# Channel products as 64-row tiles, the channel mix as four 64x64 tiles, shrinkage in 1024-column instructions

## The chip, the cores and the metric

One core of one Trainium2 chip. The metric is the device time of one launch, in microseconds (us), the median of several runs. Engines: TensorE (PE in the rows, its weight loads PEld), VectorE (DVE), ScalarE (ACT), GpSimd (POOL), SyncE (SP, which issues most DMAs here). A kernel that is better has a lower time.

## The reference

Four layers are applied to `x` of shape (8, 64, 256, 256) in float32: 8 images, 64 channels, 256 by 256 pixels.

```
# layer 0: channel attention
att = einsum('bcn,bdn->bcd', q, q)                  # the Gram matrix, q = x as (b, 64, 65536)
x   = gamma * einsum('bcd,bdn->bcn', softmax(max(att) - att), q) + x
# layers 1 and 3: a long convolution with a separable filter, plus bias * x
# layer 2: Haar wavelet, two branches of channel product and soft shrinkage, inverse Haar
f1 = haar2d(x)
for i in range(2):
    f4  = einsum('bchw,oc->bohw', f1 * v[i], conv_w[i])
    acc = acc + sign(f4) * relu(abs(f4) - tau[i])
x = haar2d(acc, inverse=True) + x
```

The convolution filters come from a small network of three sine layers, which the kernel evaluates once at its start.

## The kernel before

The images go one after the other through two kinds of stage, each of 64 steps (one per channel, or one per group of 8 image rows). `timeline` writes their order by hand: mix of image 0; forward stage -1; mix of image 1; six times a forward stage with all three parts (`fwd`, `shrink`, `gram`) and an inverse stage with mix; a forward stage without Gram (stage 6); an inverse stage without mix; `last_shrink`; a last inverse stage. `quads` unrolls four steps into a loop body and lets parts of one step work on items of earlier steps (`on[k]` is the part with lag k). All engines run the same step list and meet at counting semaphores; `CR` is an offset of 5.

**Forward stage.** In each step TensorE does, for the next image, two Toeplitz products of the first convolution (`toeplitz`, L464 and L466), a full forward Haar of one axis (`haar_fwd`, L474) and a half Haar of the other (`haar_halves`, L490, in fp32r). For the present image it multiplies the coefficients by the two channel matrices: `product(a)` for a = 0, 1 (L538). Each is two float32 matmuls whose stationary operand is 128 x 128, that is 64 channels x 2 row halves in partitions and 128 pixels as columns, and whose moving operand is `chan_w`, 128 x 256. That operand is block-sparse: `chan_w` holds each weight once per row half and a zero for the other half. `turn` (L549) transposes the same pixels with `eye`, since layer 2 adds its input. Four matmuls of a Gram product per step (L442) stand in two halves, one behind `product(1)` and one behind the second Toeplitz product. Every float32 matmul shows as two records in the trace, each with its own weight load; a transpose shows as one.

The shrinkage of a step is a chain over four engines. Before, each of its links works on one bank of 512 columns at a time: `scale(a)` (DVE, L941, multiplies by `v`), `absolute(a)` (ACT, L721, back into PSUM), `sign(a)` (ACT, L725), `less(a)` (DVE, L948, subtracts `tau` in PSUM), `relu(a)` (ACT, L730, into `mag`), magnitude times sign (POOL, L1089), the sum of the two branches (POOL, L1092, into `pair_sum`), and `field` (DVE, L971), which adds the transposed input. `product(a)` waits for `relu` of that bank from the step before; `turn` waits for `field` of the step before. ACT also evacuates the Toeplitz result into `mid` (L735), which frees bank 0 for the next step's first Toeplitz product; writes `split_b` (L756, `f_hi`), which waits for the half Haar of that step; and copies `res` (L769). DVE also makes `x1` (L980), the low part of `split_b` (L985) and two one-row corrections (L960, L961).

**Inverse stage.** Per step one fp32r inverse Haar (L482), a half Haar (L490) and two Toeplitz products. Where `mix` is on, 64 matmuls a stage (`mix_one`, L615) apply the attention matrix to the image after next: stationary `mix_w`, 128 x 128 and block-sparse in the same way, moving 512 pixels. ACT copies each result (L799) into one of two buffers and sends it to DRAM. `mix_one(m)` waits for the copy of m - 2, so the two banks alternate. Every 12 steps hold 16 of these, one or two in a step.

**last_shrink** does products, turns and shrinkage of the last image with nothing beside them. Its vector instructions have 1024 columns already (L1055, L844, L846, L1070, L841, L1116), only the branch sum (L1120) and `field` (L1064) have 512. Its products are L665.

Of the kernel before, what the change touches and what calls it, by code (L numbers as in the profile page):

```python
# [22 lines left out]
F32 = mybir.dt.float32  # L23
# [6 lines left out]
C = 64  # L30
# [87 lines left out]
def build(nc, x_pix, x_rows, gamma, zt, w1, w23, wo, b123, freq, bias, v, tau, cw, decay, signs_fwd, signs_inv,  # L118
# [4 lines left out]
    with ctx:  # L123
# [7 lines left out]
        coef = nc.dram_tensor("coef", (B, C, H, 2 * N), F32, kind="Internal").ap()  # L131
        mixed = nc.dram_tensor("mixed", (C, H, 2 * N), F32, kind="Internal").ap()
# [12 lines left out]
        held = sb("held", [128, 2, 512])  # L145
        sgn = sb("sgn", [128, 2, 512], BF16)
# [8 lines left out]
        mix_w = sb("mix_w", [128, 2 * C])  # L155
        chan_w = sb("chan_w", [128, 4 * C])
# [90 lines left out]
        def _(sp):  # L247
# [22 lines left out]
            def load_img(c, d):  # L270

                src = mixed[bass.ds(c, 1), :, :].rearrange("o p n -> p (o n)")
                sp.dma_start(img[:, d].rearrange("p a n -> p (a n)"), src).then_inc(img_in[d], 16)

            def load_coef(b, chunk, buf):

                rows_of = coef[bass.ds(b, 1), :, :, :].rearrange("o c (s t) n -> (o c s) (t n)", s=2)
# [52 lines left out]
            def inverse_stage(b, inv, mix):  # L330
                if mix:
# [3 lines left out]
                    if inv:  # L335
                        sp.wait_ge(c_pair, 128 * b + 128 + CR)
                        sp.nop(nofuse=True)
                        sp.wait_ge(c_sign, 128 * b + 128 + CR)
# [90 lines left out]
        def _(pe):  # L429
# [76 lines left out]

            def inverse_width(n, bank):
# [6 lines left out]
            def forward_stage(b, fwd, shrink, gram):  # L514
# [11 lines left out]
                def step(q, j, on):  # L526
# [3 lines left out]
                    def product(a):  # L530
                        src = crows[j // 2]
                        if j % 2 == 0 and a == 0:
                            pe.wait_ge(crows_in[j // 2], 16 * (16 * b + q) + 16)
                        pe.wait_ge(c_relu, 2 * (64 * b + d) + a - 1 + CR)
                        o_ps = ps[:, 4 + a, :].rearrange("p (i c h) -> p i c h", i=2, h=4)
                        for t in range(2):
                            at = 512 * t + N * a + H * (j % 2)
                            mm = nc.tensor.matmul(o_ps[:, :, :, 2 * t:2 * t + 2], src[:, at:at + H], chan_w[:, :],  # L538
                                                  start=True, stop=True)
                        mm.then_inc(c_mm, 1)  # L540

                    def turn():
                        src = crows[j // 2]
                        pe.wait_ge(c_field, 64 * b + d + CR)
                        for a in range(2):
                            o_ps = ps[:, 6, N * a:N * a + N].rearrange("p (c h) -> p c h", h=4)
                            for t in range(2):
                                at = 512 * t + N * a + H * (j % 2)
# [644 lines left out]
```

## Time and profile before

| | |
|---|---|
| runs | 6577.37, 6580.49, 6584.24 us; median 6580.49 us |
| the profiled execution | 6581.41 us in all, span 6579.6 us |
| TensorE busy | 6266.2 us, 95% of the span |
| mean granted clock of TensorE | 0.983 of full speed |
| VectorE, ScalarE, GpSimd busy | 61%, 59%, 39% |

The profile shows one execution. "Span" runs from the first to the last instruction. A step of a forward stage with all three parts takes 7.04 us, so a tenth of a microsecond in each of the 384 such steps is 38 us of the kernel.

### The profile page before, as it was taken

To read this page: it belongs to the slowest core of one execution; us is meant where nothing else is said; L and a number is where in the kernel's file an instruction comes from. 1 tells how busy PE (TensorE), PEld (TensorE's weight loads), DVE (VectorE), ACT (ScalarE), POOL (GpSimd) and SP (SyncE) were. 2 spreads that over 40 slices of the span, in tenths; PEclk is the share of its full clock that TensorE was granted. 3 is DMA by queue.
4 is the path that set the end of the run, shared out by engine and by line. 5 is a ranking of instruction groups with operands and counts; after the bars stand their busy time and mean duration, and the time that the engine had idled before them with its cause. 6 is when DMAs were issued, how large, how long until landed. Compare 5 with 4: busy or idle time off the path is not lost.

```text
span 6579.6 us, 140048 instructions
## 1 busy us (share of the span) xinstructions
PE 6266.2 (95%) x37984; PEld 5474.9 (83%) x37984; DVE 4017.5 (61%) x7165; ACT 3907.0 (59%) x7001; POOL 2553.6 (39%) x2436
## 2 busy tenths in 40 slices
PE   6798799999999999999999999999999999999689
PEld 4496599889998899888998889988998889988579
DVE  1142377556775577755776567755677558866866
ACT  0233466556665566655666566655666557755865
POOL 0000255324552255423553245532455226633952
PEclk9899899999999999999999999999999999999999
DMA  6676656575556655576555766666655665534224
GB/s 197 220 215 209 209 185 188 183 232 184 187 176 205 218 186 185 164 234 203 187 186 177 234 189 185 187 189 219 190 188 174 217 202 169 172 123 141 74 86 129
DMA packets 770784, 1216.81 MB, mean 185 GB/s; under 512 B 78855, under 2 KB 475048, under 8 KB 770569
## 3 DMA queue, kind: packets, MB, share of 16 engines
q1 hardware_dynamic: 623112, 945.68, 48.4%
q10 hardware_dynamic: 147456, 268.50, 10.8%
q8 instruction: 106, 1.74, 0.1%
q14 instruction: 110, 0.89, 0.0%
HBM read 808.13 MB, written 405.73 MB: 184 GB/s over the span
## 4 chain that ended last, share of the span: by engine, by line
PE 90%; DMA 4%; ACT 2%; DVE 2%; issue 1%; POOL 1%; SPq 0%; ACTq 0%; DVEq 0%; POOLq 0%
PE ps L464 27%; PE ps L466 14%; PE ps L538 12%; PE ps L482 7%; PE ps L490 7%; PE ps L474 7%; PE ps L442 7%; PE ps L615 5%; DMA mixed<-x 3%; PE ps L549 3%; PE ps L665 1%; DMA pix<-in_x_pix 1%; ACT x L799 1%; DVE pix L1055 1%; DVE ps L1070 1%
## 5 line engine op out<-in xcount | busy, mean ns | idle before, releaser
L1089 POOL TENSOR_TENSOR mag<-mag,sgn 128x512 f32<-128x512 f32 x896 | 1039.3, 1160 | 2124.0 <-ACT mag L730 2093.3
L1104 POOL TENSOR_TENSOR split_a<-field,split_a 128x512 fp32r<-128x512 f32 x512 | 651.3, 1272 | 1751.5 <-ACT split_a L782 1751.5
L464 PE MATMUL ps<-tab_a,img 128*128 128x256 f32 x4096 | 1226.5, 381 | 14.5 <-DMA img<-mixed 8.2
L464 PE MATMUL ps<-tab_b,mid 128*128 128x256 f32 x4096 | 1224.3, 381 | 0.4 <-DVE x L980 0.4
L941 DVE TENSOR_TENSOR held<-ps,v_t 128x512 f32<-128x512 f32 x896 | 619.8, 692 | 601.5 <-PE ps L538 560.5
L466 PEld LDWEIGHTS ps<-tab_a,img 128*128 128x128 f32 x4096 | 781.2, 191 | 107.4
L466 PEld LDWEIGHTS ps<-tab_b,mid 128*128 128x128 f32 x4096 | 778.8, 190 | 105.4
L466 PE MATMUL ps<-tab_a,img 128*128 128x128 f32 x4096 | 789.2, 274 | 0.0
L466 PE MATMUL ps<-tab_b,mid 128*128 128x128 f32 x4096 | 787.3, 274 | 0.0
L464 PEld LDWEIGHTS ps<-tab_a,img 128*128 128x128 f32 x4096 | 700.0, 192 | 88.6 <-DMA img<-mixed 8.5
L482 PE MATMUL ps<-s_inv,split_a 128*128 128x256 f32 x4096 | 704.2, 315 | 38.0 <-issue 37.7
L482 PEld LDWEIGHTS ps<-s_inv,split_a 128*128 128x128 f32 x4096 | 546.9, 192 | 187.9 <-issue 178.6
L1092 POOL TENSOR_TENSOR pair_sum<-mag 128x256 f32<-128x256 f32 x896 | 650.5, 726 | 103.9 <-POOL mag L1089 66.6
L756 ACT ACTIVATE split_b<-ps 128x512 fp32r<-128x512 f32 x512 | 305.7, 597 | 618.5 <-PE ps L490 609.9
L799 ACT ACTIVATE x<-ps 128x512 f32<-128x512 f32 x512 | 305.9, 598 | 586.4 <-PE ps L615 406.2
L442 PE MATMUL ps<-pix 128*128 128x128 f32 x4096 | 614.0, 277 | 26.0 <-DMA pix<-in_x_pix 26.0
L464 PEld LDWEIGHTS ps<-tab_b,mid 128*128 128x128 f32 x4096 | 627.2, 192 | 3.9 <-issue 0.6
L985 DVE TENSOR_TENSOR split_b<-ps,split_b 128x512 fp32r<-128x512 f32 x512 | 354.1, 692 | 452.4 <-ACT split_b L756 450.7
L782 ACT ACTIVATE split_a<-field 128x512 fp32r (+1 forms) x512 | 322.6, 630 | 502.6 <-PE ps L482 434.7
L948 DVE TENSOR_TENSOR ps<-ps,tau_t 128x512 f32<-128x512 f32 x896 | 619.4, 691 | 1.5 <-ACT ps L721 1.4
L735 ACT ACTIVATE mid<-ps 128x512 f32<-128x512 f32 x512 | 305.6, 597 | 520.8 <-PE ps L466 520.8
L442 PEld LDWEIGHTS ps<-pix 128*128 128x128 f32 x4096 | 564.0, 193 | 52.5 <-DMA pix<-in_x_pix 30.9
(101 smaller groups left out, 11118.1 us busy)
## 6 DMA issues: line engine op xcount, KB each, us to landing
pix<-in_x_pix SPq DMA_DIRECT2D x256, 512.0 KB, 3.8
mixed<-x ACTq DMA_DIRECT2D x512, 256.0 KB, 3.3
img<-mixed SPq DMA_DIRECT2D x512, 256.0 KB, 2.7
tab_a<-filt SPq DMA_DIRECT2D x1024, 128.0 KB, 2.8
tab_b<-filt SPq DMA_DIRECT2D x1024, 128.0 KB, 2.8
out<-res SPq DMA_DIRECT2D x512, 256.0 KB, 3.4
coef<-res ACTq DMA_DIRECT2D x496, 256.0 KB, 2.0
pix<-in_x_rows SPq DMA_DIRECT2D x128, 512.0 KB, 5.0
```

Source lines behind the costliest of these rows:

```text
L442: mm = nc.tensor.matmul(ps[:, 7, 0:2 * C], pix[:, buf, j, :], pix[:, buf, j, :], start=False, stop=False, skip_group_check=True)
L464: nc.tensor.matmul(o_ps, src[:, 0, H * half:H * half + H], tab[:, N - 1::-1], start=True, stop=False)
L466: mm = nc.tensor.matmul(o_ps[:, H:N], src[:, 1, H * half:H * half + H], tab[:, N - 1:H - 1:-1], start=False, stop=True)
L474: mm = nc.tensor.matmul(o_ps, src[:, kh, H * half:H * half + H], s_fwd[:, kh, :].bitcast(F32), start=(kh == 0), stop=(kh == 1), skip_group ...
L482: mm = nc.tensor.matmul(ps[:, bank, N * half:N * half + N], src[:, piece, kh, H * half:H * half + H], s_inv[:, kh, :], start=(kh == 0 and ...
L490: mm = nc.tensor.matmul(ps[:, bank, :], signs[:, :], src[:, piece].rearrange("p a n -> p (a n)"), start=(piece == 0), stop=(piece == 1))
L538: mm = nc.tensor.matmul(o_ps[:, :, :, 2 * t:2 * t + 2], src[:, at:at + H], chan_w[:, :], start=True, stop=True)
L941: nc.vector.tensor_tensor(held[:, a].rearrange(grouped, i=2, h=4), ps[:, 4 + a, :].rearrange(grouped, i=2, h=4), table(v_t, a), ALU.mult)\
L948: nc.vector.tensor_tensor(bank, bank, table(tau_t, a), ALU.subtract).then_inc(c_less, 1)
L1089: nc.gpsimd.tensor_tensor(mag[:, a], mag[:, a], sgn[:, a], ALU.mult).then_inc(c_mult, 1)
L1092: nc.gpsimd.tensor_tensor(pair_sum[:, a], mag[:, a, 0:N], mag[:, a, N:2 * N], ALU.add)\
L1104: nc.gpsimd.tensor_tensor(split_a[:, 1], src, split_a[:, 0].bitcast(F32), ALU.subtract)\
```

## The change

- **Products.** `chan_w` becomes 128 x 128: the plain 64 x 128 weights, once on partitions 0 to 63 and once on 64 to 127. The layout of the coefficients puts the two row halves on these two partition halves, and `row_products` makes eight matmuls of 64 rows by 128 moving columns in place of four of 128 rows by 256. The two row halves alternate and write different PSUM banks. Products of both banks stand together, first in the step.
- **Turns.** The four transposes stay, but write single float32 values with a stride of 8 (before: two neighbours with a stride of 4).
- **Mix.** `mix_w` becomes 128 x 64. Two matmuls of 128 x 128 by 512 become four of 64 x 64 by 512, one for each quarter of the array. They are issued together, once per two old slots, and wait until both banks have been copied.
- **Gram.** The four matmuls stand together behind the products. The full Haar moves ahead of the second Toeplitz product.
- **Shrinkage.** Scale, absolute, sign and less become one instruction of 1024 columns each. Less writes a new buffer `diff` in place of PSUM, and the products wait for it and no more for relu. Relu, the product with the sign and the branch sum stay at 512 and 256 columns; the branch sum writes with a stride of 8 values (32 bytes). `field` reads runs of 4 values with a stride of 8.
- **Orders.** On ACT the shrinkage comes first, then `split_b`, then `mid` (before, `mid` was first). On POOL both products with the sign stand ahead of both sums.

```diff
-                    def product(a):
+                    def products():
...
-                        pe.wait_ge(c_relu, 2 * (64 * b + d) + a - 1 + CR)
-                        o_ps = ps[:, 4 + a, :].rearrange("p (i c h) -> p i c h", i=2, h=4)
-                        for t in range(2):
-                            at = 512 * t + N * a + H * (j % 2)
-                            mm = nc.tensor.matmul(o_ps[:, :, :, 2 * t:2 * t + 2], src[:, at:at + H], chan_w[:, :],
-                                                  start=True, stop=True)
-                        mm.then_inc(c_mm, 1)
+                        pe.wait_ge(c_less, 64 * b + d + CR)
+                        row_products(4, crows[j // 2], j % 2).then_inc(c_mm, 1)
...
+            def row_products(bank, src, half):
+                for a in range(2):
+                    for t in range(2):
+                        at = 512 * t + N * a + H * half
+                        for s in range(2):
+                            o_ps = ps[:, bank + s, :].rearrange("p (i a t c) -> p i a t c", i=2, a=2, t=2)
+                            mm = nc.tensor.matmul(o_ps[:, :, a, t, :], src[C * s:C * s + C, at:at + H],
+                                                  chan_w[C * s:C * s + C, :], start=True, stop=True)
+            def row_turns(bank, src, half):
+                o_ps = ps[:, bank, :].rearrange("p (c a t s) -> p a t s c", a=2, t=2, s=2)
...
+                        mm = nc.tensor.transpose(o_ps[:, a, t], src[:, at:at + H], eye[:, :])
...
                     if shrink and on[0] and not opening:
-                        product(0)
+                        products()
+                    if gram and on[1] and not opening:
+                        gram_four()
...
-                    if shrink and on[0]:
-                        product(1)
-                    if gram and on[1]:
-                        gram_half(0)
+                    if fwd and on[2]:
+                        ...
+                        haar_fwd(2, x1[:, j % 2]).then_inc(f_mm3, 1)
                     if fwd and on[1]:
...
                         toeplitz(1, mid[:, d1 % 2], tab_b[:, d1 % 4]).then_inc(f_mm2, 1)
-                    if gram and on[1]:
-                        gram_half(1)
-                    if fwd and on[2]:
...
-                        pe.wait_ge(mix_copied, e - 1 + CR)
-                        nc.tensor.matmul(ps[:, 6 + m % 2, :], mix_w[:, :],
-                                         xrows[chunk % 4][:, 512 * (m % 2):512 * (m % 2) + 512],
-                                         start=True, stop=True).then_inc(mix_mm, 1)
+                        pe.wait_ge(mix_copied, 64 * g + 16 * r + 2 * chunk + CR)
+                        for half in range(2):
+                            for s in range(2):
+                                mm = nc.tensor.matmul(ps[C * half:C * half + C, 6 + s, :], mix_w[C * s:C * s + C, :],
+                                                      xrows[chunk % 4][C * s:C * s + C, 512 * half:512 * half + 512],
+                                                      start=True, stop=True)
+                                if half:
+                                    mm.then_inc(mix_mm, 1)
...
# ACT, forward step: the order after
+                    if shrink and on[0]:
+                        absolute_and_sign()
+                        relu(0)
...
+                    if fwd and on[2]:
+                        act.wait_ge(f_mm3, n - 1 + CR)
+                        act.wait_ge(f_mm4, n - 2 + CR)
+                        nc.scalar.activation(split_b[:, 0], halved(ps[:, 2, :]), ACT.Copy).then_inc(f_hi, 1)
+                    if fwd and on[4] and not draining:
+                        store()
                     if fwd and on[0]:
                         act.wait_ge(f_mm1, n + 1 + CR)
...
# DVE, forward step
-                        dve.wait_ge(c_abs, u + a + 1 + CR)
-                        nc.vector.tensor_tensor(bank, bank, table(tau_t, a), ALU.subtract).then_inc(c_less, 1)
+                        dve.wait_ge(c_abs, m + 1 + CR)
+                        dve.wait_ge(c_relu, 2 * m + CR)
+                        nc.vector.tensor_tensor(diff[:].rearrange("p s n -> p (s n)").rearrange(grouped, y=16), banks,
+                                                table(tau_t, q, j), ALU.subtract).then_inc(c_less, 1)
...
# POOL, forward step and last_shrink
-                        nc.gpsimd.tensor_tensor(pair_sum[:, a], mag[:, a, 0:N], mag[:, a, N:2 * N], ALU.add)\
+                        both_rows = pair_sum[:].rearrange("p a n -> p (a n)").rearrange("p (c y s) -> p s y c", y=4, s=2)
+                        nc.gpsimd.tensor_tensor(both_rows[:, s], row[:, 0], row[:, 1], ALU.add).then_inc(c_pair, 1)
...
+                    nc.gpsimd.tensor_tensor(wide_pair[:, d].rearrange("p (c y s) -> p s y c", y=4, s=2),
+                                            both[:, :, 0], both[:, :, 1], ALU.add).then_inc(c_pair, 1)
```

The DRAM layouts of `coef`, `mixed`, `x_rows`, `v` and `tau` are permuted to match. Each partition still moves 2 KB in a coefficient or mix store and in an image load, and 4 KB in a coefficient or pixel-row load.

## Rows read from the trace of the kernel before

**Rows 1.** The page's first part: engine, busy us (share) x instructions.
```profile
PE 6266.2 (95%) x37984; PEld 5474.9 (83%) x37984; DVE 4017.5 (61%) x7165; ACT 3907.0 (59%) x7001; POOL 2553.6 (39%) x2436
```

**Rows 2.** Windows: start:end us, PE, PEld, DVE, ACT, POOL busy, PEclk, DMA share.
```profile
1099.91:1106.95 7.04, 7.04 (x48) 6.50 (x47) 5.20 (x10) 4.85 (x10) 3.78 (x5) 1.00 0.65 184
400.00:404.87 4.87, 4.87 (x36) 4.57 (x35) 2.09 (x4) 1.68 (x3) 0.00 (x0) 1.00 0.74 274
5600.26:5606.40 6.14, 6.14 (x40) 5.59 (x39) 5.17 (x10) 4.84 (x10) 3.73 (x4) 1.00 0.62 184
130.00:264.00 134.00, 88.31 (x128) 26.66 (x128) 0.00 (x0) 37.61 (x63) 0.00 (x0) 0.81 0.73 242
6100.00:6300.00 200.00, 137.13 (x679) 109.25 (x677) 167.01 (x170) 170.95 (x170) 190.30 (x114) 1.00 0.23 68
```

**Rows 3.** Chain that sets the end, one forward step: start us, us, what.
```profile
1104.56 0.86 PE ps L538 x4
1105.42 0.43 PE ps L464 x2
...
1106.73 0.86 PE ps L538 x4
1107.60 0.45 PE ps L442 x4
...
1109.80 0.90 PE ps L474 x8
1110.69 0.46 PE ps L490 x2
1111.16 0.44 PE ps L549 x4
```

**Rows 4.** Timeline around changes of the matmul shape: start us, us, engine, line.
```profile
43.08 0.50 PE L442 MATMUL ps<-pix 128*128 128x128 f32 x3
43.51 0.19 PEld L454 LDWEIGHTS ps<-field 64*64 64x64 f32 x2
...
44.86 0.59 PE L454 MATMUL ps<-field 64*64 64x256 f32 x2
45.38 0.49 PE L442 MATMUL ps<-pix 128*128 128x128 f32 x2
...
2002.12 0.29 PEld L501 LDWEIGHTS ps<-eye,x 64*128 64x128 f32 x2
```

**Rows 5.** The same chain in an inverse stage: two matmuls of the mix.
```profile
1262.71 1.72 PE ps L615 x4
```

**Rows 6.** Timeline: ACT behind the half Haar; DVE behind the products.
```profile
400.56 0.60 ACT L756 ACTIVATE split_b<-ps 128x512 fp32r<-128x512 f32 x1 [2.95 <-PE ps L490]
401.06 0.59 ACT L769 ACTIVATE res<-ps 128x512 f32<-128x512 f32 x1
...
1107.83 0.69 DVE L941 TENSOR_TENSOR held<-ps,v_t 128x512 f32<-128x512 f32 x1 [0.83 <-PE ps L538]
```

**Rows 7.** The chain in last_shrink: one round of two steps.
```profile
6150.46 1.23 DVE pix L1055
...
6151.71 1.04 ACT ps L844
...
6152.86 1.25 DVE ps L1070
...
6154.12 1.03 ACT img L841
...
6155.20 2.01 PE ps L665 x8
```

**Rows 8.** Groups by line and form: busy us, mean ns of one | idle before.
```profile
L1116 POOL TENSOR_TENSOR img<-img,x 128x1024 f32<-128x1024 f32 x64 | 136.6, 2134 | 20.6 <-ACT img L841 19.8
L1120 POOL TENSOR_TENSOR mid<-img 128x512 f32<-128x512 f32 x64 | 81.0, 1266 | 9.8 <-POOL img L1116 9.5
L971 DVE TENSOR_TENSOR field<-pair_sum,ps 128x512 f32 x420 | 284.6, 678 | 0.0
```

More of the change, by code:

```diff
@@ L145, in build @@
         held = sb("held", [128, 2, 512])
+        diff = sb("diff", [128, 2, 512])
         sgn = sb("sgn", [128, 2, 512], BF16)
@@ L544, in turn, with gram_four @@
                         pe.wait_ge(c_field, 64 * b + d + CR)
[L545 to L548, printed above, removed]
[L549 to L552 removed]
+                        row_turns(6, src, j % 2).then_inc(c_copy, 1)
+                    def gram_four():
                         e = j - 1
                         uses = (GCH // 2) * (b + 2) + q + e // 2 // 2
[L555 to L556 removed]
+                        mm = gram_part(uses, (e // 2) % 2, 4 * (e % 2), 4, e % 2 == 0)
+                        if e % 2:
                             mm.then_inc(gram_chunk, 1)
@@ L569, in step @@
                             pe.wait_ge(i_res, 64 * b + CR)
-                        product(0)
-                    if shrink and on[0]:
-                        product(1)
-                    if gram and on[1]:
-                        gram_half(0)
+                        products()
+                    if gram and on[1] and opening:
+                        gram_four()
+                    if fwd and on[2]:
+                        pe.wait_ge(f_x1, n - 1 + CR)
+                        pe.wait_ge(f_lo, n - 2 + CR)
+                        haar_fwd(2, x1[:, j % 2]).then_inc(f_mm3, 1)
                     if fwd and on[1]:
@@ L750, in step @@
                     draining = isinstance(q, int) and q == 16
-                    if fwd and on[4] and not draining:
-                        store()
                     if fwd and on[2]:
@@ L756, in step @@
                         nc.scalar.activation(split_b[:, 0], halved(ps[:, 2, :]), ACT.Copy).then_inc(f_hi, 1)
+                    if fwd and on[4] and not draining:
+                        store()
+                    if fwd and on[0]:
+                        act.wait_ge(f_mm1, n + 1 + CR)
+                        act.wait_ge(f_mm2, n - 1 + CR)
+                        nc.scalar.activation(mid[:, j % 2], halved(ps[:, 0, :]), ACT.Copy).then_inc(f_mid, 1)
                     if shrink and on[0]:
@@ L1156, in layout @@
     cw = a["L2_conv_conv_w"].transpose(2, 0, 1).reshape(C, 2 * C)
-    arrays["cw"] = np.zeros((C, 2, 2 * C, 2), np.float32)
-    for s in range(2):
-        arrays["cw"][:, s, :, s] = cw
-    arrays["cw"] = arrays["cw"].reshape(128, 4 * C)
+    arrays["cw"] = np.concatenate([cw, cw], axis=0)
     t = np.linspace(0.0, 1.0, N)[::-1]
```

198 lines of the change are left out of this document (81 added, 117 removed).

## The prediction

> **What bounds the kernel now.** First the page's engine list [rows 1]: TensorE is busy 95% of the span. Then windows of single steps [rows 2]. A forward step with all three parts takes 7.04 us and TensorE is busy 7.04 of them at full clock, while DVE has 5.20, ACT 4.85 and POOL 3.78. Stage -1 (4.87 us a step) and stage 6 (6.14) are full in the same way. Then the chain that sets the end [rows 3]: in such a step it never leaves TensorE, so it is a price list. 2 x 0.86 products, 2 x 1.31 Toeplitz (1105.42 to 1106.73), 2 x 0.45 Gram, 0.90 full Haar, 0.46 half Haar, 0.44 turns: 7.04. Two stretches differ. The first mix (130 to 264 us) [rows 2] has TensorE at clock 0.81, busy 88 of 134 us, DMA share 0.73. In last_shrink POOL is busy 190 of 200 us. So microseconds must come off TensorE, and off other engines only if they become the longest.
>
> **What a matmul shape costs.** A record of 256 columns takes 0.86 / 4 = 0.216 us [rows 3], one of 128 columns 0.11 (0.45 / 4). A weight load of 128 columns needs 0.107: two of them last 0.29 where one lasts 0.19, with moving data of only 64 columns between them; two of 64 columns last 0.19 [rows 4]. Changing the tile shape is not free. The last 128 x 128 record before L454 starts at 43.08 + 2 x 0.11 = 43.30 and has streamed by 43.41, but the next load starts at 43.51: 0.10 idle, then the load itself (0.055 for 64 columns, 0.107 for 128) with nothing to hide it. Back again: L454's second record starts at 45.07, has streamed by 45.29, the load starts at 45.38 and takes 0.107. So a block of tiled matmuls pays 0.20 + 0.20 for 128-column weights and 0.15 + 0.20 for 64-column ones.
>
> **Products.** Eight matmuls are 16 records of 128 columns, eight in each row half. No row shows two row halves at once. Bounds: with both halves streaming all the time 8 x 0.108 = 0.86; with none at once 16 x 0.108 = 1.73, as before. I take the first, because the two halves use separate rows of the array, separate partitions and separate banks, and within one half a record (0.108) covers the next load (0.107). With the changes of shape a step pays 1.26 for 1.73: -0.47, step 6.57. Over 384 steps: -180 us. (Bounds over 384 steps: both unhidden changes and no overlap, +0.40 x 384 = +154; overlap and free changes, -0.87, -334.)
>
> The Trainium skill (TensorEngine Tiling, "Key Properties") says that tiles load and multiply in parallel and that changing the mode drains TensorE. No run here shows the first yet; the 0.10 us agree with the second.
>
> **Does another chain take over?** The loop of the shrinkage is products, scale, abs, less, field, turns, products: `less` now gates both the products and, through DVE's order, `field`. From [rows 3, 6, 7, 8]: change of shape 0.20, products 0.86, tail of a matmul 0.165 (its records end so much after streaming), 0.24 until scale starts (products end at 1107.59 by the chain, scale at 1107.83), scale 1.23, gap 0.02, abs 1.04, gap 0.11, less 1.16 (the next DVE instruction starts 0.09 before its end), field 0.68, gap 0.06, turns with an exposed load 0.55: 6.3 us. That is below 6.57, so the gram stages stay on TensorE with 0.25 to spare. POOL's two sums are due before less ends; by the same rows they are done about 0.9 us earlier, and only `field`, with x1 and the low part behind it on DVE, would wait for them. The 1024-column instructions save DVE and ACT a few tenths a step (two scales at 0.69 against one at 1.23) off the path: nothing by themselves; without them, and with `less` gating the products, the loop would be longer by those tenths. In stage 6 a step without Gram would be 6.14 - 0.47 = 5.67, but the loop gives 6.3: +0.16 x 64 = +10 us.
>
> **Order on ACT.** `mid` now stands behind `split_b`, which waits for the step's last half Haar. `mid` frees bank 0, for which the next step's first Toeplitz waits, and with it everything behind that on TensorE. With products and Gram ahead of it (1.26 + 0.89) this is covered. In stage -1 only the Gram (0.89) is ahead. Loop there [rows 3, 6]: 0.09 from the half Haar's end (400.47 by the chain) to `split_b` at 400.56, 0.50 to the next ACT instruction, `mid` 0.60, 0.05, an exposed load and the tail 0.27, then Toeplitz 1.31, Haar 0.90, Toeplitz 1.31, half Haar 0.46: 5.49 against 4.87. 64 x 0.62 = +40 us.
>
> **Mix.** Two old matmuls: 1.72 us [rows 5], four records of 0.43. New: four matmuls, eight records of 0.43, one matmul in each quarter, each quarter's two records one behind the other. Bounds: all four quarters at once 0.86; in order, with the next tile joining only when the second record of the last has started, 5 x 0.43 = 2.15; none at once 3.44. I take the row halves as independent and the two column halves of a row half joining in order: 3 x 0.43 = 1.29, plus 0.35 for the shapes, 1.64, -0.08. 32 x 6 = 192 such groups: -15 us. In the two stages of mix alone the copies and stores set the pace (134 us for 64, 4.2 us for two [rows 2]): nothing, up to +35 each if losing the alternation of the banks adds a matmul to each round, since that clock (0.81) is not full. The copies are otherwise ready long before the next group: a step is nearly 5 us.
>
> **last_shrink.** Its chain [rows 7] is 7.1 us for two steps, of which products are 2.01; that falls to about 1.15. But POOL needs 2134 + 1266 ns and a gap a step [rows 8], 3.5 us, and stays. Nothing. The branch sum now writes with a stride; the nearest row is the contiguous 1266, so +0; if it doubled, +81.
>
> **Strides.** The turns write single values; their old pairs cost no more (0.44 for four) than contiguous Gram (0.45). I take +0; if each were to take twice as long, 0.44 x 448 = +197. `field` reads runs of four: DVE's `field` writes with a stride today and takes 678 ns [rows 8], no more than a contiguous scale of as many columns (0.69, [rows 6]): +0. DMA sizes do not change, and the 0.65 share of a step leaves room.
>
> **Sum.** -180 + 10 + 40 - 15 = -145. The profiled execution took 6581 us, 1 above the median of 6580. So 6436, rounded 6435.
>
> **Rivals.**
> - *Strict order* (25%, slower). If TensorE starts records only in program order, a tile's second record, which must wait for its first, holds back the other tile's. Eight product matmuls then take 9 slots of 0.108 (-0.37, -142 us; stage 6 +17), and the mix 2.15 + 0.35 = 2.50 for 1.72: 192 x 0.78 = +150. With the +40: +65, 6646. It is decided by the mix: above about 1.9 us of streaming a group eats the products' gain. The Trainium skill (TensorE: Matmul & The Clock Gate, "Part 3: Packing small matmuls") has this rule: matmuls start and end in program order, and only loads are pulled ahead. For it: the consecutive starts of every chain here. Against: no row has a held-back record of one tile before another tile's.
> - *Loads one at a time* (12%, slower). A load of 128 columns takes as long as a record. If only one can run, products take 1.73 + 0.40: +146 in the gram stages, about +60 in stage 6, +40, -15 to +150 for the mix: 6810 to 6960.
> - *All four quarters at once* (20%, faster). The mix at 0.86 + 0.35 gives 192 x -0.51 = -98 for -15: 6350. If the changes of shape were hidden too, the gram step would meet the loop (6.1) and the sum go to about 6150.
> - *Single-value writes stall the turns* (8%): 6435 + 197 = 6630, slower. The Trainium skill (SBUF — State Buffer, "Door 1: The DMA port swizzle") says that any non-contiguous PSUM access slows matmuls, PSUM lines being two float32 wide; the old half-contiguous writes cost nothing, so the trace neither shows nor excludes it.
>
> **Chances.** My forecast 33%, all four at once 20%, strict order 25%, serial loads 12%, turns 8%, a change that cancels out 2%. What this kernel's measurement can tell from no change is 0.2% (13 us). The first two are faster, 53%; a mild form of the third or the last (a mix nearer 2 us, turns a little slower) adds 4%: faster 0.57, within 0.2% 0.05, slower 0.38. The range takes in 6350 and most of what lies below, and 6646 with its bounds, not the serial loads: 6270 to 6700. The likeliest case alone is 6400 to 6480.
>
> **What would show it.** Right: a gram step of 6.6 us; L-rows of the products with eight records per row half in about 0.9 us, their starts in pairs; a gap of 0.1 us and an unhidden load on each side; a mix group of 1.3 us of streaming. TensorE still without waits in gram stages; in stage -1 about 0.6 us a step of waiting for `mid`. Wrong: product records spaced 0.1 without pairs; mix groups over 2 us; turns above 0.44; POOL's sum over 1.2 us, or a step bounded by field.

## The result, and the profile after

The kernel after takes 6476.6 us (median of four runs, 6472.57 to 6480.45); the kernel before took 6578.93 us beside it on the same chip (four runs, 6577.28 to 6584.24). The ratio is 0.9843, with a 95% interval of 0.9826 to 0.986. The forecast was 6435 us: the sign and the rough size are right (-102 us for -145), but the likeliest case's own range, 6400 to 6480, holds the time only because large errors of both signs cancel. All readings below are of one profiled execution, span 6478.7 us.

The first line of the page of the kernel after answers to [rows 1]:

```profile
PE 5967.7 (92%) x43104; PEld 5135.8 (79%) x43104; DVE 3985.4 (62%) x6260; ACT 3885.0 (60%) x6105; POOL 2527.7 (39%) x2436
```

TensorE has lost 298 us of busy time and the kernel only 102: TensorE now has holes, 511 us of the span against 313. The windows of the kernel after (columns as in [rows 2]) say where: a step of stage -1, a step with all three parts, a step of stage 6, the first mix, 200 us of last_shrink.

```profile
400.46:406.39 5.93, 5.15 (x36) 4.66 (x35) 2.18 (x4) 1.68 (x3) 0.00 (x0) 1.00 0.53 181
1100.31:1106.91 6.60, 6.60 (x57) 5.97 (x56) 5.04 (x7) 4.90 (x8) 3.61 (x5) 1.00 0.66 197
5400.14:5406.43 6.29, 5.92 (x48) 5.00 (x48) 5.04 (x8) 4.72 (x7) 3.71 (x5) 1.00 0.38 125
135.00:274.00 139.00, 62.16 (x252) 10.60 (x256) 0.00 (x0) 37.02 (x62) 0.00 (x0) 0.50 0.72 227
5990.00:6190.00 200.00, 125.01 (x1134) 99.81 (x1136) 166.69 (x170) 170.99 (x170) 191.34 (x114) 0.82 0.25 71
```

The step with all three parts is full still, 0.44 us shorter. Stage -1 has grown from 4.87 to 5.93 and TensorE idles 0.78 of it. Stage 6 has grown from 6.14 to 6.29 and idles 0.37.

**The gram step.** The chain of the kernel after through one such step answers to [rows 3]:

```profile
1100.31 1.09 PE ps L515 x16
1101.40 1.09 PE ps L443 x8
...
1106.47 0.44 PE ps L525 x4
```

Products and Gram together are 2.18 where they were 2.62 (2 x 0.86 and 2 x 0.45). The chain puts a change of shape partly to the one, partly to the other; the two belong together. The turns (L525) are at 0.44 as before. How the products run is seen in TensorE's timeline of 0.55 us at the start of the block:

```profile
1100.24 0.83 PE L515 MATMUL ps<-chan_w,rows 64*128 64x128 f32 x10
```

Ten records have started in 0.55 us, where one behind the other at 0.11 would be five. The single starts in the trace are 1100.242 and .249, .456 and .462, .567 and .574, up to 1101.126 and .132: pairs 6 to 7 ns apart, 0.112 from pair to pair. The last pair has streamed at 1101.24; the Gram's first load starts at 1101.33.

**The mix.** The chain of the kernel after in an inverse stage, answering to [rows 5], and TensorE's timeline of the first 0.38 us of the same group:

```profile
2083.29 1.02 PE ps L624 x8
2084.31 1.14 PE ps L483 x8
```

```profile
2083.22 0.66 PE L624 MATMUL ps<-pix,mix_w 64*64 64x512 f32 x4
```

Four records have started where the forecast had two: starts at 2083.218, .225, .232 and .238, and the second records of the same four tiles at .698 to .718. All four quarters run at once. The 0.48 between the two is the 0.43 of a whole record and the first load, which nothing hides (0.055 by the forecast's reading of [rows 4]). So the streaming is about 0.86. The next load starts at 2084.24, 1.02 after the first, and the Haar that follows pays 1.14 for its usual 0.94, so a group costs 1.22 for 1.72. Over 12 steps of an inverse stage, with 8 groups, the time falls from 62.0 to 58.0 us.

**Stage -1.** Its chain in the kernel after:

```profile
401.04 0.04 ACT split_b L751
...
401.24 0.55 ACTq L745
...
401.96 0.61 ACT mid L757
...
402.61 0.70 PE ps L465 x2
```

The wait for `mid` is there as forecast. What stands between `split_b` (401.04) and `mid` (401.96) is 0.92 us and not 0.50: the issue of the coefficient store, on ACT's queue (L745), which the new order also puts ahead of `mid`.

**Other rows.** The strided `field` and POOL's strided sum show in the groups by line and form of the kernel after:

```profile
L958 DVE TENSOR_TENSOR field<-pair_sum,ps 128x512 f32 x420 | 284.2, 677 | 0.0
...
L1109 POOL TENSOR_TENSOR mid<-img 128x512 f32<-128x512 f32 x64 | 82.1, 1283 | 7.4 <-POOL img L1105 4.8
```

1283 for 1266 ns [rows 8], and `field` 677 for 678: the strides cost next to nothing. In last_shrink the chain of one round is

```profile
6049.56 1.24 DVE pix L1044
...
6054.31 2.10 PE ps L515 x16
...
6056.64 1.23 DVE pix L1044
```

7.08 us for two steps, as before. The products did not fall to 1.15: the granted clock of this stage is 0.82 (1.00 before, [rows 2]), and these run near the lower of the two levels. It costs nothing, since POOL is busy 191 of the 200 us, as forecast.

**Where the 101 us are.** From the times of the first and last record of each block in both traces (span to span, 6579.6 to 6478.7):

| stretch | before, us | after, us | difference |
|---|---|---|---|
| start to first product (two mixes alone, stage -1) | 749.5 | 832.5 | +83 |
| of this stage -1 | 304.5 | 369.5 | +65 |
| of this the two mixes alone | 131.7, 133.7 | 139.3, 139.2 | +13 |
| six cycles of a gram stage and an inverse stage | 6 x 776.3 | 6 x 743.0 | -200 |
| stage 6, first product to first inverse Haar | 398.7 | 415.2 | +16 |
| the rest | | | -1 |

Inside a cycle: 64 x -0.44 = -28.2 for the products; about -14 in the inverse stage (312.0 to 297.6 from its first Haar to its last on the mean of six, with the mix); and two things that no step of the forecast has. On the mean of the six gram stages it takes 19.6 us for 15.1 from the first product to the first Haar of the stage, and 14.6 (14.3 to 15.1) for 11.2 from the last product to the first inverse Haar. The second table below takes these up.

### The profile page after: what moved, and what is told of

It reads as the page before. It is cut to its first block, busy times and chain, and to the rows that moved or that the text cites. A ratio compares the mean times of both kernels' runs of the same rounds, so it can differ in the third digit from the quotient of the medians.

```text
span 6478.7 us, 146006 instructions
## 1 busy us (share of the span) xinstructions
PE 5967.7 (92%) x43104; PEld 5135.8 (79%) x43104; DVE 3985.4 (62%) x6260; ACT 3885.0 (60%) x6105; POOL 2527.7 (39%) x2436
## 4 chain that ended last, share of the span: by engine, by line
PE 85%; ACT 3%; DMA 3%; DVE 3%; issue 3%; ACTq 1%; POOL 1%; SPq 0%; DVEq 0%; POOLq 0%
PE ps L465 27%; PE ps L467 14%; PE ps L515 8%; PE ps L483 8%; PE ps L475 7%; PE ps L491 7%; PE ps L443 7%; PE ps L624 4%; PE ps L525 3%; DMA mixed<-x 2%; ACT x L800 1%; DVE pix L1044 1%; DMA pix<-in_x_pix 1%; DVE field L958 1%; ACT ps L845 1%
## 5 line engine op out<-in xcount | busy, mean ns | idle before, releaser
L465 PE MATMUL ps<-tab_a,img 128*128 128x256 f32 x4096 | 1248.3, 387 | 91.6 <-ACT mid L757 77.3
L467 PEld LDWEIGHTS ps<-tab_a,img 128*128 128x128 f32 x4096 | 786.0, 192 | 109.3
L465 PEld LDWEIGHTS ps<-tab_a,img 128*128 128x128 f32 x4096 | 664.9, 193 | 158.4 <-ACT mid L757 58.3
L935 DVE TENSOR_TENSOR held<-ps,v_t 128x1024 f32<-128x1024 f32 x448 | 548.5, 1224 | 370.1 <-PE ps L515 370.1
L950 DVE TENSOR_TENSOR diff<-ps,tau_t 128x1024 f32<-128x1024 f32 x448 | 548.8, 1225 | 299.5 <-ACT ps L722 299.5
L731 ACT ACTIVATE mag<-diff 128x512 f32<-128x512 f32 x896 | 561.4, 627 | 256.5 <-DVE diff L950 256.5
L483 PEld LDWEIGHTS ps<-s_inv,split_a 128*128 128x128 f32 x4096 | 530.5, 194 | 209.8 <-issue 193.1
L483 PE MATMUL ps<-s_inv,split_a 128*128 128x256 f32 x4096 | 625.9, 296 | 44.1 <-issue 39.7
L965 DVE SCALAR_TENSOR_TENSOR x<-img,bias,ps 128x512 f32<-128x512 f32 x512 | 382.1, 746 | 443.3 <-PE ps L467 441.4
L722 ACT ACTIVATE ps<-held 128x1024 f32<-128x1024 f32 x448 | 460.7, 1028 | 289.1 <-DVE held L935 289.0
L443 PE MATMUL ps<-pix 128*128 128x128 f32 x4096 | 586.3, 288 | 26.3 <-DMA pix<-in_x_pix 26.3
```

What stands on the lines that cost most here:

```text
L443: mm = nc.tensor.matmul(ps[:, 7, 0:2 * C], pix[:, buf, j, :], pix[:, buf, j, :], start=False, stop=False, skip_group_check=True)
L465: nc.tensor.matmul(o_ps, src[:, 0, H * half:H * half + H], tab[:, N - 1::-1], start=True, stop=False)
L467: mm = nc.tensor.matmul(o_ps[:, H:N], src[:, 1, H * half:H * half + H], tab[:, N - 1:H - 1:-1], start=False, stop=True)
L483: mm = nc.tensor.matmul(ps[:, bank, N * half:N * half + N], src[:, piece, kh, H * half:H * half + H], s_inv[:, kh, :], start=(kh == 0 and ...
L722: nc.scalar.activation(pair_of_banks(2), held[:].rearrange("p s n -> p (s n)"), ACT.Abs)\
L731: nc.scalar.activation(mag[:, s], diff[:, s], ACT.Relu).then_inc(c_relu, 1)
```

## Experiments

Each ran in three rounds or more beside the kernel before, whose median was 6577 to 6580 us every time; "after" is 6476.6 us. The edits are shown abbreviated.

### Do the row halves give the products' gain?

**Eight products of whole rows.** The same eight matmuls and the same order, but each 128 rows high, with weights that hold zeros for the other row half. Nothing changes shape.

```diff
-  mm = matmul(o_ps[:, :, a, t, :], src[C*s:C*s+C, at:at+H], chan_w[C*s:C*s+C, :])
+  mm = matmul(o_ps[:, :, a, t, :], src[:, at:at+H], chan_w[:, 2*C*s:2*C*s+2*C])   # chan_w [128, 4*C], zero-padded
```

> The changed kernel, with its eight product matmuls a step on the whole array: 128 rows of stationary operand against weights that are zero for the other row half. Same banks, waits and neighbours; no change of tile shape. Theory (the two row halves streamed at once, 0.84 us for 16 records, and each change of shape costs 0.2 us): products 16 x 0.11 = 1.75 us for 1.29, the gram step 6.60 to about 7.06 us, 384 x 0.46 = +177, stage 6 bound by the shrinkage loop (6.29 + 0.6 = 6.9) +40: about 6690 us. Rival (the time came off from the new order and the shorter vector instructions, the tiles give nothing): within 15 us of 6477.

Measured: 6719.85 us, ratio 1.0215 (1.0198 to 1.0232). Its chain has

```profile
1700.94 1.79 PE ps L515 x16
1702.72 0.89 PE ps L443 x8
```

2.68 against 2.18, step 7.10 us. The concurrency of the two row halves, less what the changes of shape cost, is worth 243 us here; the new layout with whole matmuls would have lost 141 to the kernel before.

**One row half behind the other.** The eight matmuls as in the change, but all four of one row half first.

```diff
-  for a in range(2):
-      for t in range(2):
-          for s in range(2):
+  for s in range(2):
+      for a in range(2):
+          for t in range(2):
```

> The changed kernel, with the eight product matmuls issued as four of row half 0 and then four of row half 1, in place of alternating. Theory that each row half has an order of its own and TensorE looks far ahead: records of both halves still start in pairs, within 10 us of 6477. Rival (records may pass each other only over a short distance, or not at all when more than one stands in the way): products up to 1.73 + 0.4 = 2.1 us, the gram step bound by the shrinkage loop, 6.3 + 0.85 = 7.15: about +0.55 x 384 = +210 and +55 in stage 6, 6740 us.

Measured: 6759.57 us, ratio 1.0277 (1.026 to 1.0294), step 7.14. The chain, and TensorE's timeline of the same 0.55 us as above:

```profile
1705.10 1.64 PE ps L515 x16
```

```profile
1705.03 0.93 PE L515 MATMUL ps<-chan_w,rows 64*128 64x128 f32 x6
```

Six starts and not ten. The single starts: the first half's records at 1705.029, .243, .354, .466 and .578, and only then, at .584, the first record of the second half. From there the two halves run side by side until the first ends, and the second finishes alone, its last record starting at 1706.467. (The rows do not name the half; this assignment is the one in which each half has eight records.) So the order is not strict: the second half's first matmul starts while the second record of the first half's third matmul and its whole fourth, which stand ahead of it, have not. But here it started no earlier than beside the fifth record, so the two halves ran together for part of the block only; alternating in the program, they did from the first record on. The same work in another order of three loops costs 283 us, 210 of them in the gram steps; stage 6 and last_shrink are 36 and 34 us longer.

The Trainium skill (TensorE: Matmul & The Clock Gate, "Part 3: Packing small matmuls") has matmuls start in program order with only weight loads pulled ahead. Here a matmul started ahead of an earlier one, the fourth of the first half. The forecast's rival of strict order is excluded by the kernel after alone: it had 0.97 us of streaming for the products and 2.15 for the mix, and they take 0.89 and about 0.86.

**What a change of shape costs.** Products, Gram and products again: two more changes a step each way.

```diff
+  row_products(4, crows[j // 2], j % 2, (0,))
+  gram_four(0, 1)
+  row_products(4, crows[j // 2], j % 2, (1,)).then_inc(c_mm, 1)
+  gram_four(1, 3)
```

> The changed kernel, with the products of a gram step in two blocks of four matmuls and one of the four Gram matmuls between them: two more changes of tile shape a step, no more work. Theory (a change of shape costs 0.10 us of empty array and an exposed load of 0.107): +0.40 us a step, gram step 7.0 us, 384 x 0.40 = +154, 6630 us. Rival (the empty time is hidden by work of the other shape, or TensorE had slack in these steps): within 20 us of 6477.

Measured: 6627.24 us, ratio 1.0077 (1.006 to 1.0094), step 7.00 us. The chain:

```profile
1704.62 0.65 PE ps L515 x8
1705.26 0.42 PE ps L443 x2
1705.68 0.65 PE ps L515 x8
1706.32 0.86 PE ps L443 x6
```

2.58 against 2.18: +0.40 for one more block, the 0.20 + 0.20 that the forecast read from [rows 4]. The whole gain of the row tiles would be gone with two blocks a step, so putting both products together is part of what makes the change pay.

### What the four quarters give

**Mix whole, with a two-level store.** `mix_w` block-diagonal again, two matmuls of 128 x 128, everything else as after. The output rows then come in another order, which the store set right by a pattern with two entries outermost.

```diff
-  destination pattern [[per_c, 128], [1, 512]]
+  destination pattern [[2 * C * per_c, 2], [per_c, C], [1, 512]]
```

> The changed kernel, with the mix as two matmuls of 128 x 128 by 512 and a block-diagonal weight, issued at the same places and with the same waits. Theory (four quarters stream at once, 0.95 us a group, plus 0.35 for the shapes, against 1.72): +0.4 to +0.5 us for each of 192 groups, +77 to +96, and up to +15 in the two stages of mix alone: 6555 to 6590 us. Rival (inverse stages became shorter for another reason): under 6500.

Measured: 8105.26 us, ratio 1.2324, outside everything expected, and no verdict on the mix. The chain in the first mix:

```profile
198.88 10.62 DMA mixed<-x
```

A store of 256 KB takes 10.62 us from its issue to landing; in the kernel after the same chain shows 3.4 to 3.6. The bytes and the sizes of the contiguous pieces are the same. The Trainium skill (DMA: Bandwidth & Descriptors, "Rules for kernel authors") says that a transfer uses no more DMA engines than its outermost dimension has entries, here two of sixteen. The tripled time agrees in direction; no row here counts the engines of one transfer.

**Mix whole, plain store.** The same, with the host's layout of the pixel rows permuted so that the store keeps its old pattern.

```diff
-  CHUNKS, 2, 2).transpose(0, 5, 1, 4, 6, 3, 2)
+  CHUNKS, 2, 2).transpose(0, 6, 1, 4, 5, 3, 2)
```

> The mix as two whole matmuls again, now with the pixel rows laid out so that each store of the mix is the same plain pattern of 128 rows as in the changed kernel; all else as changed. Theory (four quarters at once, 0.95 us and 0.35 for the shapes, against 1.72): +77 to +96 us over 192 groups, up to +15 in the two stages of mix alone: 6555 to 6590 us. Rival (the inverse stages became shorter for another reason, and the slowness of the first try was more than its store): under 6500, or still over 7000.

Measured: 6566.57 us, ratio 0.9982 (0.9972 to 0.9992). A group is 1.72 again, and the inverse stage 312.3 us on the mean of six (312.0 before, 297.6 after):

```profile
2084.95 1.72 PE ps L623 x4
```

So the quarters are worth 90 us of the 102. The forecast gave them 15.

### The order on ACT

**`mid` ahead of everything in stage -1.**

```diff
+  mid_first = not shrink
+  if fwd and on[0] and mid_first:
+      make_mid()
```

> The changed kernel, with mid again the first instruction of ACT's step where there is no shrinkage (stage -1 only). Theory (the new order on ACT puts mid behind split_b, which waits for the step's last half Haar; the loop takes 5.93 us a step for 4.88 of work): stage -1 back to 4.88 us a step, -65 us: 6412. Rival (stage -1 is held up by the Haar standing ahead of the second Toeplitz, or by loads): within 10 us of 6477.

Measured: 6414.07 us, ratio 0.9751 (0.9735 to 0.9767). The chain never leaves TensorE there and the step is 4.87 (401.57 to the next Gram):

```profile
401.10 0.47 PE ps L491 x2
401.57 0.89 PE ps L443 x8
```

**Only the store behind `mid`.**

```diff
-  if fwd and on[4] and not draining: store()
   if fwd and on[0]: mid
+  if fwd and on[4] and not draining: store()
```

> The changed kernel, with the issue of the coefficient store moved behind mid on ACT in all forward stages; mid stays behind split_b. Theory (the issue of the DMA, 0.55 us and its register work, is part of the loop of stage -1 and is what the forecast of 5.49 left out): stage -1 at 5.5 us a step, -27 us: 6450. Rival (the issue runs beside the ACT instruction and costs nothing): within 5 us of 6477.

Measured: 6439.9 us, ratio 0.9791 (0.9774 to 0.9807). The steps of stage -1 are 5.41 and 5.47: the forecast's loop of 5.49, which left out the store's issue, was right for this order. Stage -1 falls from 369.5 to 341.9 us by the store's place alone, and from there to 306.3 by that of `mid`; the rest of this run's gain lies in the other stages, 1.8 us a cycle (741.3 for 743.0).

**`mid` first in the first two steps of a shrink stage.** The opening of a gram stage, in the chain of the kernel after:

```profile
1575.98 1.12 PE ps L515 x16
...
1577.12 1.24 DVE held L935
...
1579.44 1.23 DVE diff L950
...
1581.23 0.59 ACT mid L757
...
1581.95 1.19 PE ps L465 x2
...
1584.85 2.00 PE ps L515 x16
```

`mid` here waits behind the whole shrinkage of the first item, since nothing older is in flight. TensorE stands until 1581.95. Then the records cost about double: 2.00 for products that are 1.09 elsewhere. The windows of the kernel after show the granted clock in this stretch:

```profile
1577.12:1581.95 4.83, 0.54 (x4) 0.32 (x5) 2.45 (x2) 3.26 (x5) 0.55 (x1) 0.78 0.72 218
1584.85:1586.86 2.01, 2.01 (x18) 1.82 (x17) 0.00 (x0) 0.00 (x0) 0.19 (x1) 0.55 0.01 2
```

TensorE was busy 0.54 of the 4.83 us, and in them the clock has gone to its lower level, 1.2 GHz; the products run almost wholly at that level.

```diff
+  mid_first = shrink and isinstance(q, int) and q == 0 and j < 2
```

> The changed kernel, with mid ahead of the shrinkage on ACT in the first two steps of each forward stage alone. Theory (in the first step TensorE has only Toeplitz and products; its next Toeplitz waits for mid, and mid waits behind abs, sign and relu of the first products; TensorE stands idle for 5 us and comes back at half clock): each of seven stages starts 4 us earlier, -28 us: 6449. Rival (the second products wait for less anyway, so the start costs the same): within 8 us of 6477.

Measured: 6444.18 us, ratio 0.9794 (0.9779 to 0.9809), 32 us less than after. The same two blocks of products in its chain:

```profile
1572.74 1.12 PE ps L515 x16
...
1577.48 1.19 PE ps L515 x16
```

The second follows after 4.7 us and not 8.9, and the clock stays full. From first product to first Haar it takes 14.2 us in most stages (19.2 after, 14.9 before), and a cycle 737.6 for 743.0.

### Stage 6 and the 1024-column instructions

The loop that the forecast summed to 6.3 us is seen in the timelines of DVE and TensorE in stage 6. It comes back to `field` each 6.31, and each link starts on the end of the one before it:

```profile
5405.04 0.68 DVE L958 TENSOR_TENSOR field<-pair_sum,ps 128x512 f32 x1
5405.77 0.66 PE L525 MATMUL ps<-eye,rows 128*128 128x128 f32 x4 [0.37 <-DVE field L958]
...
5407.70 1.23 DVE L935 TENSOR_TENSOR held<-ps,v_t 128x1024 f32<-128x1024 f32 x1 [0.62 <-PE ps L515]
...
5410.21 1.23 DVE L950 TENSOR_TENSOR diff<-ps,tau_t 128x1024 f32<-128x1024 f32 x1 [0.64 <-ACT ps L722]
5411.35 0.68 DVE L958 TENSOR_TENSOR field<-pair_sum,ps 128x512 f32 x1
```

The profile's own chain puts TensorE's Toeplitz products ahead of `field` in this stage. By the timeline `field` stands right behind `less` on DVE. The two runs below test the loop.

**Scale, absolute and less in halves of 512 columns.** The forecast held that 1024 columns keep this loop short. Its rival: a link of 1024 columns hands nothing on until all are done, and lengthens the loop.

```diff
-  act.wait_ge(c_scaled, m + 1 + CR)
-  activation(pair_of_banks(2), held, ACT.Abs)
+  for s in range(2):
+      act.wait_ge((h_scaled, c_scaled)[s], m + 1 + CR)
+      activation(ps[:, 4 + s, :], held[:, s], ACT.Abs)
   # the same for scale and less; relu(s) waits for its own half
```

> The changed kernel, with scale, absolute and less again in two instructions of 512 columns, one for each bank, so that the second of one engine runs beside the first of the next; sign, waits of the products and orders as changed. Theory of the forecast (shorter busy time is what keeps the loop short): the loop gets longer, stage 6 over 6.3 us a step, +10 to +30 us. Rival (the loop counts latency, and halves overlap: scale to field 3.3 us for 4.25): stage 6 falls from 6.3 to TensorE's own 5.7 us, the gram steps stay at 6.60: -38 us and a little at each start of a stage, 6435.

Measured: 6438.99 us, ratio 0.9788 (0.9772 to 0.9805). The steps of stage 6 are 5.95 us. The halves cost DVE 63 us of busy time more and ACT 41 less in the page's sums, and take 38 us off the kernel. The steps of stage 6 are 22 of them (64 x 0.35). A cycle is 2.6 us shorter as well, nearly all of it in the openings (16.7 for 19.6 us), so the 6435 expected by the rival was met with steps longer than its 5.7. The step does not get to 5.67, what TensorE's own work takes, because a second loop closes at 5.95. It is the one of stage -1, with the issue of the store (ACTq) and `mid` at its end:

```profile
5399.79 0.49 PE ps L492 x2
...
5400.58 0.56 ACTq L746
...
5401.31 0.61 ACT mid L758
...
5401.96 0.70 PE ps L466 x2
```

**Turns of stage 6 one step later**, with 1024 columns kept, so that they never wait for `field`.

```diff
+  late = shrink and not gram
+  if late and on[1] and not opening:
+      turn(1)
-  if shrink and on[0]:
+  if shrink and on[0] and not late:
```

> The changed kernel, with the turns of stage 6 one step later, right behind the next products, so that they are no link of the shrinkage loop (products, scale, abs, less, products remain, about 5.2 us). Theory (stage 6 is bound by the loop through field and turns, 6.3 us): TensorE's own 5.7 us a step, -38 us: 6439. Rival (a second loop, DVE's order or POOL's sums, stands right behind, as the 5.95 us with 512-column instructions hints): 5.95 us a step, -22 us: 6455.

Measured: 6454.11 us, ratio 0.9807 (0.9792 to 0.9822). Again steps of 5.94, and TensorE's timeline names the same wait:

```profile
5402.73 0.60 ACT L763 ACTIVATE mid<-ps 128x512 f32<-128x512 f32 x1 [0.34 <-issue]
5403.38 0.30 PEld L465 LDWEIGHTS ps<-tab_a,img 128*128 128x128 f32 x2 [0.25 <-ACT mid L763]
```

Two different cures of the first loop stop at the same second one.

### The mix alone

**Two pairs of banks in turn** in the two stages of mix alone, to see whether losing the alternation of the banks costs the 13 us.

```diff
-  pe.wait_ge(mix_copied, 64*g + 16*r + 2*chunk + CR)
+  pe.wait_ge(mix_copied, 64*g + 16*r + 2*chunk - (0 if inv else 2) + CR)
+  bank = 6 if inv or chunk % 2 == 0 else 4
```

> The changed kernel, with the mix of the two stages without an inverse part going to PSUM banks 4 and 5 and banks 6 and 7 in turn. Theory (these stages became longer by 6 to 8 us each, and TensorE fell to half clock there, because a group now waits for both banks to be copied): back to 132 us each, -13 us: 6464. Rival (copies and stores of 4.3 us for two results set the pace, TensorE is hidden at either clock): within 5 us of 6477.

Measured: 6468.99 us (6456.6 to 6473.25), ratio 0.9833 (0.9818 to 0.9848): 8 us less than after, with intervals that overlap widely: by the medians, inconclusive. In the profiled execution, the fastest of its four, the two stages take 118.8 and 134.9 us (139.3 and 139.2 after). In both kernels the chain there is a store and a copy in turn; in this one

```profile
180.79 3.26 DMA mixed<-x
```

3.1 to 3.3 us a store, for 3.4 to 3.6 in the kernel after. The granted clock is 0.51 here too.

The traces of the other runs say more. In the ten of the kernel after and its variants that wait for both banks (all but this run, the last one and the one with the slow store) the two stages take 138.6 to 143.5 us each, and mix whole is one of them, with 140.3 and 143.5 us at a granted clock of 0.75 and 0.76. So neither the quarters nor the half clock lengthens these stages. The two runs with four banks have 118.8, 134.9, 134.5 and 133.5 us (131.7 and 133.7 before). That points to the wait for both banks; why the first of the four is so short is not known.

### All together

**Mended.** `mid` first in stage -1 and in the openings, the store behind `mid` elsewhere, late turns in stage 6, four banks for the mix alone, and 512 columns for scale, absolute and less.

> All of these at once on the changed kernel: mid first in stage -1 and in the first two steps of the others, the store behind mid elsewhere, late turns in stage 6, four banks for the mix alone, and scale, absolute and less in 512 columns. If the losses are in separate places, they add up: -62 (measured for stage -1), -28, -9 (the store's part outside stage -1), -40 for stage 6, -13: 6325 us. If they overlap or TensorE finds another wait: 6360 or more.

Measured in five rounds: 6315.31 us (6308.3 to 6320.75), ratio 0.9597 (0.9584 to 0.961). It beats the kernel before by 264 us and the kernel after by 161. From its first Haar to its last, stage -1 takes 306.3 us and stage 6 355.0 (396.5 after, 383.6 before), at 5.66 us a step, with `mid` no longer in the chain:

```profile
5303.21 1.09 PE ps L516 x16
...
5304.89 0.43 PE ps L466 x2
...
5308.87 1.09 PE ps L516 x16
```

The single gains against the kernel after (62.5, 32, 38, 22.5 and, unsure, 8) add up to 163, nearly what the whole brings. The store's place outside stage -1, about 10 us alone, is not in that sum, so the parts do not add up exactly.

## Why the prediction was right and wrong

| step of the forecast | forecast, us | found, us | how known |
|---|---|---|---|
| products, 384 gram steps | -180 | -169 | step 7.04 to 6.60; whole rows +243 |
| mix, 192 groups | -15 | -90 | mix whole 6566.6 |
| ACT's order in stage -1 | +40 | +65 | `mid` first -62.5 |
| loop in stage 6, without its opening | +10 | +13 | steps 6.3; end |
| openings of seven stages | none | +30 | `mid` first there -32 |
| ends of the six gram stages | none | +21 | traces alone |
| mix alone, two stages | 0, to +70 | +13 | traces; there with mix whole, not with four banks |
| last_shrink, strides, turns | 0 | 0 | rows above |

The terms found add to -117; the traces say -101. Of the 16 us left, 5 lie ahead of the first product and 11 in the six cycles; they were not followed.

That the time fell inside the 6400 to 6480 of the likeliest case is luck. The mix gave 75 us more than its term, and the other lines took 119 back: 25 at ACT's order, 30 at the openings, 21 at the ends, 13 at the mix alone, 11 at the products, 3 in stage 6, and the 16.

**Products: right.** Pairs of starts, 0.89 of streaming, 0.40 of changes of shape. The size is 0.03 a step off, since the records came at 0.112 and not 0.108. The rival of loads one at a time is excluded: loads of the two row halves start 7 ns apart as their records do.

**Mix: the step that failed most.** It took "the row halves as independent and the two column halves of a row half joining in order". The two column halves join as freely as the row halves. That was the rival "all four quarters at once", which had -98 for it; it was given 20% and is what happened, though its total of 6350 is 127 us too low, for the losses below. Nothing in the trace of before could decide it, and the forecast took a value between its bounds for which no row gave a reason. The mechanism had to be taken alike for rows and columns, or left as two cases.

**Order on ACT: right mechanism, a term left out.** The loop was summed with "0.50 to the next ACT instruction" from [rows 6], a gap read from a kernel in which the store's issue stood elsewhere. The new order moves that issue too, 0.55 us on ACT's queue. With the store behind `mid` the steps are 5.41 to 5.47, the forecast's 5.49.

**Openings: missed.** The forecast looked at steady steps only. In the first step of a stage the shrinkage of the first item is the only thing in flight, `mid` stands behind all of it, TensorE is busy 0.5 of 4.8 us and runs on at half clock for some microseconds. The run with `mid` first there returns all of it.

**Ends of the stages: missed.** The last item's shrinkage has nothing beside it. From its last product to the end of its `field` it takes 10.8 to 10.9 us for 7.9 in every gram stage, and on DVE `x1` and the low part, for which the last Haar waits, stand behind `field`. The forecast named just this queue and gave it no price at the end of a stage. With the store behind `mid` it is 10.4 to 10.5. No run took the rest of the wait away, so it is a reading. The long instructions are not its cause: with scale, absolute and less in 512 columns the stretch is 10.8 to 10.9 us too. The chain passes there through POOL's two products and two sums (1999.5 to 2004.6 us), whose order the change also altered; no run tested that. The rest, 0.6 to 1.3 us a stage, goes with the granted clock (0.50 here), as at this last Haar in the chain of the kernel after:

```profile
2006.73 2.07 PE ps L475 x8
```

In the run with `mid` first in the openings the clock is full here. The same Haar takes 1.13, and from the last product to the first inverse Haar it is 13.7 or 13.8 us in all six stages.

**Stage 6: right.** 6.3 us forecast, 6.3 measured. But the sentence beside it, that without 1024 columns "the loop would be longer by those tenths", is false. Two instructions of 512 columns take longer than one of 1024 (2 x 0.69 against 1.23), yet the next engine starts on the first half. The loop is a matter of latency, not of busy time: halves took at least 0.35 us off it, down to where the second loop closes.

**Mix alone.** The bounds (0 to +35 each) held, the value did not: 7.6 and 5.5 us. The traces point to the forecast's own reason, the lost alternation of the banks, and not to the clock (mix whole and four banks above); the medians do not settle it.

**Two sums of the rivals** do not come out as written. Nine slots of 0.108 with 0.40 are 0.36 less than 1.73 and not 0.37, and the terms of *Loads one at a time* reach to 6976 and not 6960. Neither changes the argument.

## What to carry to other kernels

Small float32 matmuls in different row parts of the array ran at once through the whole block when they alternated in the program, and only in part when they did not (the same was not tried for column parts); keep them in one block, because each block costs 0.35 to 0.40 us of drain and unhidden load. When one engine's order is rewritten, sum the loop with every instruction that now stands ahead of the one that others wait for, DMA issues too, and do it again for the first and the last step of a stage, where nothing older covers it. Merging two vector instructions saved busy time on DVE (63 us) and added latency: on an engine that is not full, inside a loop that sets the pace, the merge was a loss.

## What the runs showed of the hardware beyond what was expected

- Two records in two row halves start 6 to 7 ns apart, four in four quarters 20 ns from first to last; four quarter matmuls of 512 columns take 1.22 us with both changes of shape, where two whole ones take 1.72.
- The look-ahead across tiles had a limit: with eight records of one half ahead, the other half's first started beside the fifth.
- The granted clock was lower where the same work was done sooner: the mix alone had 0.75 with TensorE busy 87 of 139 us (mix whole), and 0.50 with 62 of 139 (four quarters). There it is off the path; in the openings it was on it.
- A store whose outermost dimension has two entries took 10.6 us where the same bytes took 3.5.
- Transposes that write single float32 values with a stride of 32 bytes run as fast as those that write pairs, 0.44 us for four. The Trainium skill (SBUF — State Buffer, "Door 1: The DMA port swizzle") would have them slower; here they are not.
